# Loading the first three chunks of an adjacency matrix tile by tile, in a two-layer graph kernel

## What is computed

```python
scale = sum(d_list * filt * d_list, axis=0)
x = layernorm(x + adj @ (scale[:, None] * (adj @ (x @ weight))) + bias)
X_in  = (adj   / rowsum(adj))   @ x @ W_in
X_out = (adj.T / rowsum(adj.T)) @ x @ W_out
x = layernorm(x + X_in + X_out)
```

## Time and profile before

| | before |
|---|---|
| median of three runs | 736.01 us |
| the profiled execution | 736.04 us, of which its span 734.2 us |
| TensorE (PE) busy | 725.7 us, 99% |
| VectorE (DVE) busy | 616.3 us, 84% |
| ScalarE (ACT) busy | 535.8 us, 73% |
| HBM traffic | 228.56 MB, mean 311 GB/s |

### The profile page before, as it was taken

How to read it: one execution, slowest core, us unless ns; L and a number is a source line. 1 busy time by engine, 2 the same in 40 slices (tenths; PEclk the granted TensorE clock), 3 DMA queues, 4 the chain that set the end, 5 groups by cost and what they waited for, 6 DMA issues and landing times.

```text
span 734.2 us, 9297 instructions
## 1 busy us (share of the span) xinstructions
PE 725.7 (99%) x3289; PEld 600.2 (82%) x3289; DVE 616.3 (84%) x782; ACT 535.8 (73%) x1366; POOL 18.7 (3%) x15
## 2 busy tenths in 40 slices
PE   9999999999999999999999999999999999999997
PEld 5878888888888887888888888888888888888885
DVE  6899998765657899998786778998898999899996
ACT  6888888855646649467474547999989898877673
POOL 0121140000000000000000000000000000000000
PEclk9999999999999999999999999999999999999999
DMA  9999999955437878677647469999989999999991
GB/s 370 426 427 422 426 424 380 360 200 194 141 146 254 324 270 297 217 272 258 229 173 254 156 220 380 386 388 389 368 327 389 385 366 381 386 362 347 355 354 48
DMA packets 36973, 228.56 MB, mean 311 GB/s; under 512 B 3776, under 2 KB 8640, under 8 KB 9664
## 3 DMA queue, kind: packets, MB, share of 16 engines
q1 hardware_dynamic: 36656, 227.85, 80.8%
q10 hardware_dynamic: 272, 0.13, 0.1%
HBM read 225.87 MB, written 2.10 MB: 310 GB/s over the span
## 4 chain that ended last, share of the span: by engine, by line
PE 91%; DVE 5%; DMA 2%; ACT 1%; issue 0%; POOL 0%; SPq 0%; DVEq 0%; ACTq 0%
PE accB L723 13%; PE accB L718 12%; PE accB L713 12%; PE accA L718 11%; PE accA L713 11%; PE accA L723 11%; PE accC L723 6%; PE accC L718 6%; PE accC L713 6%; PE nat L772 3%; DVE lo L466 2%; DMA raw<-in_adjT_b 2%; DVE turned L526 1%; DVE rows L566 0%; ACT hi L327 0%
## 5 line engine op out<-in xcount | busy, mean ns | idle before, releaser
L466 DVE TENSOR_TENSOR lo<-raw,hi 128x2048 fp32r<-128x2048 f32 (+2 forms) x263 | 490.4, 1892 | 70.5 <-ACT hi L322 58.6
L322 ACT ACTIVATE hi<-raw 128x512 fp32r<-128x512 f32 x512 | 315.3, 622 | 63.4 <-DMA raw<-in_adjT_b 38.1
L713 PE MATMUL accA<-hi,x_hi 128*128 128x512 f32 x384 | 150.5, 392 | 0.0
L718 PE MATMUL accA<-hi,x_lo 128*128 128x512 f32 x384 | 149.4, 389 | 0.0
L327 ACT ACTIVATE hi<-raw 128x512 fp32r<-128x512 f32 x190 | 104.2, 622 | 18.7 <-DMA raw<-in_adjT_b 18.7
L723 PE MATMUL accA<-lo,x_hi 128*128 128x512 f32 x384 | 107.8, 389 | 0.0
L713 PE MATMUL accB<-hi,v_hi 128*128 128x512 f32 x256 | 99.9, 390 | 0.0
L718 PE MATMUL accB<-hi,v_lo 128*128 128x512 f32 x256 | 99.6, 389 | 0.0
L322 ACT ACTIVATION_READ_ACCUMULATOR hi<-raw 128x1 f32 x512 | 97.5, 190 | 0.0
L723 PEld LDWEIGHTS accA<-lo,x_hi 128*128 128x128 f32 x384 | 72.1, 188 | 14.9
L713 PEld LDWEIGHTS accA<-hi,x_hi 128*128 128x128 f32 x384 | 72.1, 188 | 14.6
(11 more groups left out here) (102 smaller groups left out, 525.0 us busy)
## 6 DMA issues: line engine op xcount, KB each, us to landing
raw<-in_adjT_b SPq DMA_DIRECT2D x149, 1024.0 KB, 5.3
raw<-in_adj_b SPq DMA_DIRECT2D x64, 1024.0 KB, 5.7
rows<-in_x_b SPq DMA_DIRECT2D x8, 256.0 KB, 8.3
out<-rows SPq DMA_DIRECT2D x7, 256.0 KB, 5.9
out<-rows SPq DMA_DIRECT2D x1, 128.0 KB, 1.8
out<-rows ACTq DMA_DIRECT2D x1, 128.0 KB, 2.1
coef<-in_coef_t SPq DMA_DIRECT2D x1, 96.0 KB, 8.9
w<-in_W SPq DMA_DIRECT2D x1, 64.0 KB, 8.3
```

The costliest lines, as they stand in the source:

```text
L322: nc.scalar.activation(hi[slot][:, t], raw[slot][:, t], ACT.Copy, accum_out=to[:, TPB * K + t, C:C + 1]).then_inc(s_hi, 1)
L466: nc.vector.tensor_tensor(lo[slot][:, at], raw[slot][:, at], hi[slot][:, at], ALU.subtract).then_inc(s_lo, 1)
L713: nc.tensor.matmul(acc, r_hi[:, TPB * K + t], h[:, t], start=(first and t == 0), stop=False)
L718: nc.tensor.matmul(acc, r_lo[:, TPB * K + t], h[:, t], start=False, stop=False)
```

## The change

Three things are changed.

1. Chunks 0, 1 and 2 are each loaded by four transfers of one tile (256 KB, 128 pieces of 2048 bytes) instead of one of 1 MB (128 pieces of 8192 bytes), each with a semaphore of its own. ScalarE makes hi of all their tiles, tile after tile as they land; VectorE's two copies for chunk 0 are gone, and it makes lo of these chunks by single tiles. The warming products are 7 instead of 13.
2. `x_load[2]` is 11 instead of 12: SyncE issues block 2 of x before chunk 11 instead of before chunk 12, and ScalarE splits it before chunk 11.
3. The normalisation of block 5 stands after `low` of n = 78 instead of 76 on VectorE (`x1_block`, `x1_parts`), and `deviation` after n = 79 instead of 76 on ScalarE.

```diff
-WARM = 13
+WARM = 7
+FIRST = 3
...
-    x_load = [x_from[b] - (1 if b != 2 else 0) for b in range(NB)]
+    x_load = [x_from[b] - 1 for b in range(NB)]
...
-    parts = [TPB if n == 0 else 2 if n < LEAD * NB else 1 for n in range(N4)]
+    parts = [TPB if n < FIRST else 2 if n < LEAD * NB else 1 for n in range(N4)]
...
-        landings[slot] += 16
+
+        landings[slot] += 16 if n >= FIRST else 0
...
-        hi_at.append([hi_count + (t // 2 if n == 0 else t if n < LEAD * NB or with_sums(n) else 0) + 1
+        hi_at.append([hi_count + (t if n < LEAD * NB or with_sums(n) else 0) + 1
...
+                if n < FIRST:
+                    for t in range(TPB):
+                        sp.dma_start(raw[n][:, t], adjT_b[a, b, :, t]).then_inc(s_first[n][t], 16)
+                    return
...
+                if n < FIRST:
+                    for t in range(TPB):
+                        act.wait_ge(s_first[n][t], 16)
+                        nc.scalar.activation(hi[slot][:, t], raw[slot][:, t], ACT.Copy).then_inc(s_hi, 1)
+                    return
...
-                    if n == (N1 + 4 if I == NB - 1 else last2[I] + (5 if I == NB - 2 else 4)):
+                    if n == (N1 + 4 if I == NB - 1 else last2[I] + (5 if I == NB - 2 else 7 if I == NB - 3 else 4)):
                         deviation(NB - 1 - I)
...
-                dve.wait_ge(s_raw[0], landed[0])
-                for t in (0, 2):
-                    nc.vector.tensor_copy(hi[0][:, t], raw[0][:, t]).then_inc(s_h0, 1)
...
-                    if n == last2[I] + 4:
+                    if n == last2[I] + (6 if I == NB - 3 else 4):
                         x1_block(I)
                         x1_parts(I)
```

More of the change, by code:

```diff
@@ L223, in graph_kernel @@
         s_raw = [sem(f"raw_loaded{r}") for r in range(RING)]
+        s_first = [[sem(f"tile{t}_of_chunk{n}_loaded") for t in range(TPB)] for n in range(FIRST)]
         s_st = sem("out_stored")
@@ L240, in graph_kernel @@
         s_x0 = sem("parts_of_x_block_0_ready")
-        s_h0 = sem("hi_of_chunk_0_by_vector")
         s_lo = sem("lo_ready")
@@ L324, in split @@
                 elif n < LEAD * NB:
-                    for t in range(TPB) if n else (1, 3):
+                    for t in range(TPB):
                         nc.scalar.activation(hi[slot][:, t], raw[slot][:, t], ACT.Copy).then_inc(s_hi, 1)
@@ L461, in low @@
                     at = slice(size * k, size * (k + 1))
[L462 to L465, removed]
+                    dve.wait_ge(s_hi, hi_at[n][size * (k + 1) - 1])
                     nc.vector.tensor_tensor(lo[slot][:, at], raw[slot][:, at], hi[slot][:, at],
@@ L708, in by_hi @@
                 h = hi[slot_of[n]]
-                if n == 0 and t % 2 == 0:
-                    pe.wait_ge(s_h0, t // 2 + 1)
-                elif n == 0 or t == 0 or hi_at[n][t] > hi_at[n][t - 1]:
+                if t == 0 or hi_at[n][t] > hi_at[n][t - 1]:
                     pe.wait_ge(s_hi, hi_at[n][t])
```

## The result

The changed kernel takes 737.12 us (median of 20 executions, 736.33 to 737.68), the kernel before 736.05 (20 executions, 735.82 to 736.38). The ratio is 1.0013, with a 95% interval of 1.0007 to 1.0019: 1.07 us slower, less than the 0.2% that was set as "within", but outside the range of 733.6 to 736.0, where 734.45 was forecast.

What follows compares the result with a forecast made beforehand. TensorE was taken to bound the kernel: first product, fixed stream of products, stops and an untouched tail. 736.04 - 0.24 (parts 1 and 2) - 1.35 (part 3) = 734.45 us, with a range of 733.6 to 736.0.

Steps and rivals of the forecast that it cites:

- What bounds the kernel: Whole kernel: TensorE's time is first product, fixed stream of products, two stops and an untouched tail; TensorE busy 725.7 of 734.2 us.
- Part 3: At the lo products of chunk 77: moving block 5's norm later removes TensorE's stop, winning 1.35 us.
- 0.25 us in hand at n = 85: Behind the norm of block 4: VectorE's lo of n = 85 still comes 0.25 us before TensorE needs it, no new stop.
- Part 2: At chunk 12: loading block 2 of x sooner removes TensorE's 0.66 us stop on GpSimd; chunk 11 then lands later.
- d: At the start: how far cutting the first three chunks moves the queue's loads; taken as 0.3 us, ends -0.2 and 0.8.
- The instruction packet: Near chunk 10: an instruction fetch delays one DMA engine's share some 1.4 us; assumed to come again at about the same place.
- rival C: The instruction fetch comes after chunk 11, so the feed no longer decides there: 734.0 us; chance 0.14.
- Part 1: At the start: first product 1.7 us sooner through tile loads, but worth at most 0.30 us at the end.
- What is d?: First three chunks: 2048-byte pieces cost 0 to 0.067 us a tile, 0.4 for twelve, less 0.1 won at the start.
- Rival D: First three chunks: small transfers one behind another are slow, 1.0 us a tile, 4.7 us in all: 738.85 us; chance 0.10.
- The stop at chunk 11: At chunk 11: TensorE waits 0.42 us on the DMA, as 0.65 us of x goes before that chunk.
- Rival F: First chunk: clock at 1.2 GHz after fewer warming products, 0.36 us left at chunk 11: 734.8 us; chance 0.06.

Runs made afterwards that it cites:

- parts 2 and 3 alone: The kernel before with block 2 of x loaded one chunk sooner and the norm of block 5 later, first chunks whole, 13 warming products: 734.21 us.
- after: The changed kernel, all three changes against the kernel before: 737.12 us median, 736.72 us in the profiled execution.
- the other layouts: Changed kernel, 13 warming products, first chunks from copies: tiles in a row 735.46 us, tiles from 10240-byte rows 735.63, 1 MB transfers in 2048-byte pieces 735.70.
- either copy: Changed kernel, 13 warming products, first three chunks' tiles read from a copy: each tile 256 KB in a row, 735.46 us; rows padded to 10240 bytes, 735.63 us.
- part 1 alone: The kernel before with the first three chunks loaded tile by tile and 7 warming products, nothing else: 739.04 us.
- part 2 alone: The kernel before with block 2 of x loaded one chunk sooner, nothing else: 735.52 us.
- part 3 alone: The kernel before with the norm of block 5 later, nothing else: 734.69 us.

## Why the prediction was wrong

**What bounds the kernel: right.** The account of first product, stream, stops and tail holds to 0.1 us in parts 2 and 3 alone, and to 0.3 us in after. That a sooner start is worth nothing where chunk 3 is late held too: the first product came 1.19 us sooner and brought nothing.

**Part 3: right.** -1.35 forecast, -1.29 to -1.36 measured alone (by which executions of before are taken). The 0.25 us in hand at n = 85 are 0.27.

**Part 2: right.** -0.54 forecast with d = 0, -0.46 to -0.53 measured alone.

**The instruction packet: came again.** Chunk 10 is still late, split after 1.21 us of idle time (1.62 before), and one packet of instructions is again on its queue, between 30 and 32 us; rival C fell. That the packet delays the chunk was not tested.

**Part 1, the step "What is d?": wrong, and it is the whole miss.** The sum took d = 0.3 with ends of -0.2 and 0.8; the trace has 16.21 - 13.55 = 2.66. Put into the same formula, 736.04 + 2.66 - 0.54 - 1.35 = 736.81, against 736.72 in the profiled execution and 737.12 in the median. That it comes this near is in part luck, as the formula puts the end behind a late chunk 11, and the stop was at chunk 3. The step took the cost of 2048-byte pieces as so much a tile, from blocks 1 and 3 of x, and put 0.033 us down. Inside the series that isn't contradicted: eight more tiles cost nothing to 0.1 us each. What it lacked is a cost that comes where the series of cut transfers begins: four cut tiles already cost about 2.0 us in the fastest execution. Pieces of 2048 bytes in the other layouts cost 1.2 to 1.5 us in all. It also took 0.1 us as won at the start, from chunk 0's landing. The rows that it had could not show the loss: a block of x is one such transfer between large ones, its 2048-byte pieces lie in a row in memory, and the only sign of trouble, 262 GB/s at 3.0 to 3.5 us, was put down to the start-up of large pieces. Rival D had the mechanism in part, small transfers one behind another, but as a price for each of twelve tiles (4.7 us in all, 738.85), and with a chance of 0.10. The true case lay between it and the forecast, and the range, which gave the bounds of d only to 0.8, ended at 736.0.

**The stop at chunk 11: wrong with it.** It was forecast as 0.42 us on the condition that the feed is on time at the start. With d = 2.66 TensorE itself is late, chunk 11 waits for nothing, and the stop moved to chunk 3, where the list has 0.8 us.

**Rival F: happened, and its price depends on the feed.** Its evidence against, a granted clock of 1.00 at 3.0 us, was none. The column shows 1.00 also in after at 8 to 12 us, although the products there are 0.43 us apart until 10.5; the spacing of products is the better witness. The Trainium skill (TensorE: Matmul & The Clock Gate, section Part 1: The HAM clock gate) had the low clock as the resting state, and the trace agrees: with whole chunks and 7 warming products, TensorE waits 2.4 us for chunk 0, and the clock is at half from 8 to 10 us. The price was put at 0.36 us; behind the late feed it is 0.17, and without it 1.23.

**Long pieces against short ones.** The Trainium skill (Perfetto Trace Analysis, section DMA Optimizations) says that joining transfers from 2 KB to 4 or 8 KB can improve throughput dramatically. Inside the series of chunks 1 and 2 the trace disagrees (417 GB/s from 8 to 12 us, against 428 with whole chunks); at its beginning it agrees (216 against 419). It should have weighed more against a d that ended at 0.8.

**What stays open.** Why the DMA is slow where a series of cut transfers begins, why tiles out of the matrix cost about twice as much as those out of either copy when chunk 0 is cut too (with chunk 0 whole it is 1.60), and why it is still 1.25 us with tiles in a row. Each hole was seen in one profiled execution a kernel, and its place varies: in the kernel with part 1 alone the chunk 3 of its trace is at 17.28, later than in after, with the same transfers.

## What to carry to other kernels

Before a load is cut to start sooner, ask whether the start sets the end: here the next whole chunk did, and a sooner first product was worth nothing. The price of a form of transfer must be taken from a series of it in the same layout, for one such transfer between large ones doesn't show what the beginning of a series costs. When two suspected causes can hide each other, as the clock and the feed here, hold one at its good value while the other is measured, and look in the trace whether it stayed there. When a copy in another layout is compared with the original, a copy in the same layout belongs beside it.

## What the runs showed of the hardware

2048-byte pieces 10240 bytes apart in a copy instead of 8192 apart in the matrix gave 1.32 us back. A copy with 8192 is missing, so the distance is the likely cause, not the shown one.

Transfers over 32 partitions moved 221 GB/s with the DMA engines busy throughout. The Trainium skill (SBUF — State Buffer, section Door 1: The DMA port swizzle) says that 32 partitions reach 8 of 16 ports, and puts the limit near 218 GB/s; the trace agrees with the rate.

A short hole behind the warming products costs the clock in some executions and not in others. With part 2 alone the profiled execution is the one that took 737.82 us. A late chunk 0 (7.25) left TensorE idle for 1.5 us, and its stretch shows half the clock:

```profile
8.00:9.00 1.00, 1.00 (x3) 0.81 (x3) 1.00 (x3) 0.41 (x1) 0.00 (x0) 0.50 0.99 418
```

With part 3 alone chunk 0 was as late (7.09) and TensorE idle for 1.3 us, but the clock stayed:

```profile
8.00:9.00 1.00, 1.00 (x6) 0.83 (x5) 1.00 (x3) 0.25 (x1) 0.00 (x0) 1.00 0.99 418
```

The same with stops further on: in the changed kernel with 13 warming products, after a stop of 1.4 us, the products were still 0.23 us apart, and with only chunk 0 cut, after stops of 1.4 and 1.3 us, they were 0.43 apart.
